# A mixer whose B products for one half pair in eight move to TensorE, and whose C products are divided anew

## The reference

```
x, z  = split(centred(inp) @ W_in)          # 1024 channels each
u     = silu(conv4(x) + conv_b)
B, C  = split(u @ W_x)                      # 16 columns each, per token
delta = softplus(u @ W_dt + b_dt)
h[d,s] = exp(delta[d] * A[d,s]) * h[d,s] + (delta[d] * u[d]) * B[s]     # token by token
y[d]  = sum_s h[d,s] * C[s]  + u[d] * D[d]
out   = (y * silu(z)) @ W_out + residual
```

## Time and profile before

| | |
|---|---|
| median of 3 runs | 5179.13 us (5176.7 to 5179.95) |
| profiled execution | 5180.01 us, span 5178.2 us |
| mean granted TensorE clock | 0.972 |
| TensorE busy | 4693.1 us, 91%, 23936 instructions |
| VectorE busy | 4584.5 us, 89%, 7668 |
| GpSimd busy | 3878.2 us, 75%, 1637 |
| ScalarE busy | 3753.9 us, 72%, 9592 |
| first scan to last scan | about 712 to 4560 us |

### The profile page before, as it was taken

The page is one execution under the profiler, slowest core; times in us unless marked ns, Lnnn a source line. Parts: engine busy times, 40 slices in busy tenths (PEclk is TensorE's granted clock), DMA queues, the critical chain, the costliest instruction groups (busy, mean ns, idle before and its releaser), DMA issues. The chain is left out here.

```text
span 5178.2 us, 79404 instructions
## 1 busy us (share of the span) xinstructions
PE 4693.1 (91%) x23936; PEld 3776.5 (73%) x23936; DVE 4584.5 (89%) x7668; ACT 3753.9 (72%) x9592; POOL 3878.2 (75%) x1637
## 2 busy tenths in 40 slices
PE   8999988898888988898899888888988989789999
PEld 6778767777777777777777777777777777668887
DVE  6777669999999999999999999999999999977775
ACT  5656557888787888888788887878888788744443
POOL 1111059999999999999999999999999999931110
PEclk9999999999999999999999999999999999989999
DMA  3222231111111111111111111111111111111111
GB/s 84 89 83 75 109 106 43 52 46 46 54 58 54 50 46 46 46 46 46 50 55 46 46 54 56 56 50 46 46 46 46 46 46 47 65 61 49 66 57 41
DMA packets 137375, 291.88 MB, mean 56 GB/s; under 512 B 23280, under 2 KB 40688, under 8 KB 136944
## 3 DMA queue, kind: packets, MB, share of 16 engines
q1 hardware_dynamic: 136944, 286.75, 16.4%
HBM read 218.53 MB, written 68.18 MB: 55 GB/s over the span
## 5 line engine op out<-in xcount | busy, mean ns | idle before, releaser
L977 POOL TENSOR_TENSOR mx_dbu<-mx_bs,mx_du 128x2048 f32<-128x2048 f32 (+1 forms) x513 | 2327.2, 4537 | 120.9 <-DVE mx_hp L1276 120.6
L1193 ACT ACTIVATE mx_ps_da<-mx_dl,mx_a 128x256 f32<-128x256 f32 x4096 | 1776.3, 465 | 99.0 <-DVE mx_hp L1276 61.6
L1276 DVE TENSOR_TENSOR_SCAN mx_ps_da<-mx_ps_da,mx_hst,mx_dbu 128x256 f32<-128x256 f32 x2016 | 1405.5, 737 | 125.1 <-ACT mx_ps_da L1193 106.9
L1276 DVE TENSOR_TENSOR_SCAN mx_hp<-mx_ps_da,mx_hst,mx_dbu 128x256 f32<-128x256 f32 x1568 | 1145.6, 731 | 11.5 <-ACT mx_ps_da L1193 11.5
L995 POOL TENSOR_TENSOR mx_hp<-mx_hp,mx_cs 128x1024 f32<-128x1024 f32 (+1 forms) x512 | 1069.4, 2095 | 1.3 <-ACT mx_hst L1117 1.3
L1396 PE MATMUL mx_ps_m<-mx_u,mx_w_dt 128*128 128x256 f32 x4096 | 930.8, 381 | 2.7 <-issue 2.7
L1396 PEld LDWEIGHTS mx_ps_m<-mx_u,mx_w_dt 128*128 128x128 f32 x4096 | 762.9, 191 | 95.7 <-issue 3.3
L1378 PE MATMUL mx_ps_m<-mx_hT,mx_w_in 128*128 128x256 f32 x2048 | 554.0, 417 | 279.7 <-DVE mx_u L1254 279.4
L1289 DVE TENSOR_TENSOR mx_hc<-mx_ps_da,mx_cs 128x512 f32<-128x512 f32 x1024 | 683.5, 667 | 2.8 <-issue 1.9
L1378 PEld LDWEIGHTS mx_ps_m<-mx_hT,mx_w_in 128*128 128x128 f32 x2048 | 395.9, 203 | 389.8 <-DVE mx_u L1254 330.5
L1426 PEld LDWEIGHTS mx_ps_y<-mx_ident,mx_hp 128*128 128x128 f32 x3584 | 444.5, 143 | 321.5 <-POOL mx_hp L995 174.8
(11 more groups left out here) (126 smaller groups left out, 7440.4 us busy)
## 6 DMA issues: line engine op xcount, KB each, us to landing
mx_bs<-bc_scratch SPq DMA_DIRECT2D x128, 512.0 KB, 4.3
mx_cs<-bc_scratch SPq DMA_DIRECT2D x128, 512.0 KB, 3.7
mx_hT<-hT_scratch SPq DMA_DIRECT2D x32, 518.0 KB, 4.1
hT_scratch<-f_h2T SPq DMA_DIRECT2D x16, 1024.0 KB, 8.9
mx_xo<-xs_scratch SPq DMA_DIRECT2D x32, 512.0 KB, 3.7
x_scratch<-mx_xo SPq DMA_DIRECT2D x32, 512.0 KB, 2.9
f_x<-in_L_attn_inp SPq DMA_DIRECT2D x12, 1024.0 KB, 6.5
xs_scratch<-f_x SPq DMA_DIRECT2D x12, 1024.0 KB, 4.3
```

Of the source, the lines that this page charges most:

```text
L977: G.tensor_tensor(dbu[:, n % NM:n % NM + k].rearrange("p n s t -> p (n s) t"), bs[:, g:g + k].rearrange("p n s t -> p (n s) t"), bcast(du[ ...
L1193: ins = A.activation(ps_da[DA_BANK[p]][:, k, :], dl[:, b % NL, :], ACT.Exp, scale=a_sb[:, b, s:s + 1])
L1276: ins = V.tensor_tensor_scan(da if in_psum(p) else hp[:, n % NH, k, :], da, dbu[:, n % NM, s, :], 0.0 if first else hst[:, b, SG * g + s:S ...
```

## The change

Pairs with g = 2 (n = 2, 6, 10, ... 30, eight a chunk) get their first half's B times delta u from TensorE:

- `turn_du`: at step 4b - 1 TensorE transposes delta u of block b (two transposes) into a `ps_m` bank; in the last chunk's last two blocks into `ps_c`.
- `copy_du`: at step 4b ScalarE copies it to SBUF (`duT`), behind the first tap and ahead of the second half's decays. The dt product of block b + 2 now waits for this copy, as it takes the same bank.
- `load_bT`, `b_diagonals`: SyncE loads the two B columns with tokens on partitions, behind the store of B and C and ahead of the spreads; at the end of step 31 ScalarE makes four diagonal matrices, identity times a B column.
- `b_times_du`: at step 4b + 1 TensorE multiplies turned delta u by the diagonals, straight into the half's `ps_da` bank, once the half three before has been scanned.
- That half's decays go to SBUF (`da_sb`), one step earlier, and its scans read decay from SBUF and B-times-du from PSUM. They write PSUM as before.
- GpSimd's double B product leaves these two states out (1536 columns, not 2048).

Apart from this `ALL_IN_PSUM` becomes empty: GpSimd makes all the C products of second halves, and `times_c_second` is no longer used.

```
-        ALL_IN_PSUM = (4, 5, 20, 21)
+        ALL_IN_PSUM = ()
+        ON_PE = 2
+        S_PE = SG * ON_PE
+        DU_TURN_AT = [NG * b - 1 for b in range(ND)]
+        DU_COPY_AT = [NG * b for b in range(ND)]
+        DIAG_AT = [-1]
+        DBU_AT = [NG * b + ON_PE - 1 for b in range(ND)]
+        def on_pe(p):
+            return p % 2 == 0 and p // 2 % NG == ON_PE
+        def du_bank(c, b):
+            return ps_c if isinstance(c, int) and c == LAST and b >= ND - 2 else ps_m[b % 2]
# SyncE, behind the wait for the stored B and C
+            def load_bT():
+                for k in range(SD):
+                    sp.dma_start(bT[:, k, :], bc_dram[S_PE + k, :].rearrange("(j p) -> p j", p=P),
+                                 allow_slow_non_contiguous=True).then_inc(s_bt, 16)
# GpSimd, times_b
+                skip = SD if on_pe(2 * n) else 0
+                G.tensor_tensor(dbu[...].rearrange("p n s t -> p (n s) t")[:, skip:, :],
+                                bs[...].rearrange("p n s t -> p (n s) t")[:, skip:, :],
+                                bcast(du[:, b % 2, :], k * SG - skip), ALU.mult).then_inc(s_m1, k)
# ScalarE
+            def copy_du(c, b):
+                act.wait_ge(s_dut, ND * c + (b + 1))
+                if not (is0(c) and b == 0):
+                    act.wait_ge(s_db, ND * c + b)
+                A.activation(duT[...], du_bank(c, b)[:, 0:T], ACT.Copy).then_inc(s_duc, 1)
+            def b_diagonals(c):
+                act.wait_ge(s_bt, 16 * SD * (c + 1))
+                if not is0(c):
+                    act.wait_ge(s_db, ND * c)
+                for j in range(TJ):
+                    for k in range(SD):
+                        ins = A.activation(bdiag[:, j, k, :], ident[:, :], ACT.Copy, scale=bT[:, k, j:j + 1])
+                ins.then_inc(s_bd, 16)
...
                     for half in range(2):
                         p = 2 * n + half
-                        if in_psum(before(p)):
+                        if on_pe(p):
+                            pass
+                        elif in_psum(before(p)):
                             keep_psum(i, p)
+                            decay(i, p)
                         else:
                             bank_scanned(i, p)
+                            decay(i, p)
...
+                    if on_pe(2 * n + 2):
+                        decay(i, 2 * n + 2)
# VectorE, scan
+                if on_pe(p):
+                    if k == 0:
+                        dve.wait_ge(s_db, ND * i + b + 1)
+                    da, db = da_sb[:, k, :], bank
+                else:
+                    da, db = bank, dbu[:, n % NM, s, :]
# TensorE; turn_du and b_times_du stand first in their steps
+                if not (is0(c) and b < 2):
+                    pe.wait_ge(s_duc, ND * c + (b - 1))          # in dt_product
+            def turn_du(c, b):
+                ...
+                    pe.wait_ge(s_zc, ND * c + (b + 3))
+                pe.wait_ge(s_du, ND * c + (b + 1))
+                for j in range(TJ):
+                    ins = M.transpose(du_bank(c, b)[:, j * P:(j + 1) * P], du[:, b % 2, j * P:(j + 1) * P], ident[:, :])
+                ins.then_inc(s_dut, 1)
+            def b_times_du(c, b):
+                n = NG * b + ON_PE
+                if b == 0:
+                    pe.wait_ge(s_bd, 16 * (c + 1))
+                pe.wait_ge(s_duc, ND * c + (b + 1))
+                pe.wait_ge(s_sc, 2 * NU * c + (2 * n - 2))
+                for j in range(TJ):
+                    ins = M.matmul(ps_da[DA_BANK[2 * n]][:, :, j * P:(j + 1) * P], duT[:, j, :], bdiag[:, j, :, :],
+                                   start=(j == 0), stop=(j == TJ - 1), skip_group_check=True)
+                ins.then_inc(s_db, 1)
```

More of the change, by code:

```diff
@@ L726, in mixer_phase @@
         yt = sb("yt", [P, 2, T])
+        da_sb = sb("da_sb", [P, SD, T])
+        duT = sb("duT", [P, TJ, P])
+        bT = sb("bT", [P, SD, TJ])
+        bdiag = sb("bdiag", [P, TJ, SD, P])
         ps_y = [ctx.enter_context(nc.psum_tensor(f"mx_ps_y{n}", [P, 512], F32)) for n in range(2)]
@@ L757, in mixer_phase @@
         s_m1 = sem("dbu_ready")
+        s_dut = sem("du_turned")
+        s_duc = sem("turned_du_copied")
+        s_bt = sem("b_columns_loaded")
+        s_bd = sem("b_diagonals_ready")
+        s_db = sem("dbu_in_psum")
         s_da = sem("da_ready")
@@ L917, in _ @@
             sp.wait_ge(s_bcd, 16)
+            load_bT()
             for g in range(NG):
@@ L1109, in log, with decay @@
                 A.activation(en[:, b % 2, :], en[:, b % 2, :], ACT.Ln, bias=1.0).then_inc(s_sp, 1)
+            def copy_du(c, b):
+                act.wait_ge(s_dut, ND * c + (b + 1))
+                if not (is0(c) and b == 0):
+                    act.wait_ge(s_db, ND * c + b)
+                A.activation(duT[:, :, :].rearrange("p j d -> p (j d)"), du_bank(c, b)[:, 0:T], ACT.Copy).then_inc(s_duc, 1)
+            def b_diagonals(c):
[6 more added lines that the diff above has]
+                ins.then_inc(s_bd, 16)
+            def decay(i, p):
+                n, half = divmod(p, 2)
+                b, g = divmod(n, NG)
+                dst = da_sb if on_pe(p) else ps_da[DA_BANK[p]]
+                for k in range(SD):
+                    s = SG * g + SD * half + k
+                    ins = A.activation(dst[:, k, :], dl[:, b % NL, :], ACT.Exp, scale=a_sb[:, b, s:s + 1])
+                ins.then_inc(s_da, 1)
             def keep(c, n):
@@ L1172, in prologue @@
                         A.preload_act_table_set("silu_and_others")
+                    for b, c in due_before(DIAG_AT, n):
+                        b_diagonals(c)
                     for k, c in due_before(U_SILU_AT, n):
@@ L1202, in body @@
                                 skip(i + s, (par + s) % 2, bb)
+                            for bb, s in due(DU_COPY_AT, n, i):
+                                copy_du(i + s, bb)
+                    if on_pe(2 * n + 2):
+                        decay(i, 2 * n + 2)
                     if n >= KEEP_LAG:
@@ L1221, in body @@
                         log(i + s, bb)
+                    for bb, s in due(DIAG_AT, n, i):
+                        b_diagonals(i + s)
                     if due(Z_SILU_AT, n, i):
@@ L1274, in scan @@
                 s = SD * half + k
-                da = ps_da[DA_BANK[p]][:, k, :]
-                ins = V.tensor_tensor_scan(da if in_psum(p) else hp[:, n % NH, k, :], da, dbu[:, n % NM, s, :],
+                bank = ps_da[DA_BANK[p]][:, k, :]
+                if on_pe(p):
[4 more added lines that the diff above has]
+                    da, db = bank, dbu[:, n % NM, s, :]
+                ins = V.tensor_tensor_scan(bank if in_psum(p) else hp[:, n % NH, k, :], da, db,
                                            0.0 if first else hst[:, b, SG * g + s:SG * g + s + 1], ALU.mult, ALU.add)
@@ L1429, in turn_onto @@
                 return ins
+            def turn_du(c, b):
+                if isinstance(c, int) and c == LAST and b >= ND - 2:
+                    pe.wait_ge(s_o, TJ * LAST)
+                    if b == ND - 1:
+                        pe.wait_ge(s_duc, ND * LAST + b)
+                else:
+                    pe.wait_ge(s_zc, ND * c + (b + 3))
[13 more added lines that the diff above has]
+                ins.then_inc(s_db, 1)
             def sum_psum_states(c, n):
@@ L1458, in prologue @@
             def prologue():
+                pe.wait_ge(s_id, 2)
                 for n in range(EARLIEST, 0):
+                    for b, c in due_before(DU_TURN_AT, n):
+                        turn_du(c, b)
                     for b, c in due_before(DT_AT, n):
@@ L1481, in body @@
                             last_out_product(j, range(2 * k, 2 * k + 2))
+                    for b, s in due(DU_TURN_AT, n, i):
+                        turn_du(i + s, b)
+                    for b, s in due(DBU_AT, n, i):
+                        b_times_du(i + s, b)
                     for part, s in due(OUT_AT, n, i):
```

12 lines of the change are left out of this document (4 added, 8 removed).

## The result

The changed kernel takes 5208.86 us (median of 5, 5205.88 to 5210.51) against 5179.13 (5176.7 to 5183.92): ratio 1.0055, 95% interval 1.0041 to 1.0070. It is slower by about 30 us. The sign was forecast, and the place; the size, +62 us, was twice too large, though the time lies inside the range given.

The account below looks back on a forecast made before the run. VectorE's in-order list, fed by ScalarE, was taken as the bound. Chunks at +2.15 us undisturbed and +2.55 disturbed, weighted 2.3, less 0.3, gave 2.0 x 31 = +62 on 5180.0: 5242 us, range 5195 to 5295.

Parts of the forecast that it names:

- place 2: Step 16, second half: input product of step 15 comes late, delaying tap and decays; VectorE stands 2.45 us.
- undisturbed chunk: A chunk without the low clock at gate 9: forecast +2.15 us in sum.
- The disturbed chunks: 12 of 29 chunks, low clock at gate 9: step 16 wait 4.15 us in place of 1.29; chunk +2.55.
- the chunk's start: Pair 0: 0.3 us gained from GpSimd, 0.2 lost waiting for second-half decays; net 0.
- the four first chunks: First chunks of a sequence: shorter scans, less cover for TensorE, but GpSimd waits go; taken at the same sum.
- SiLU blocks: Before second halves of pairs 6 and 22: VectorE's saved time becomes waiting for ScalarE's gapless chain; -0.3 to -0.4 us a chunk.
- GpSimd: Its work falls by net 4.0 us a chunk, worth 0.3 at the chunk's start and at most 0.6.
- By gate 21 TensorE has caught up: Behind step 16: B-times-du of step 17 ends some 2 us early enough; TensorE's lateness is gone by gate 21.
- Scans with exchanged operands: VectorE's scans with the two operands' places exchanged keep their present 0.73 us; +-0.02 on 16 scans is +-0.3.
- The copy: ScalarE's copy of turned delta u, between tap and second-half decays: 362 ns each, +0.36 us in place 2.
- The B column loads: SyncE's two loads ahead of the B spreads: cost nothing; a few us at each chunk's start if both took 7.4.
- the estimate: ScalarE's four diagonals of 128 columns: 0.28 us each, +1.1 a chunk, bounds 0 and 1.45.

Follow-up runs that it names:

- e1: Changed kernel with TensorE's output parts moved to steps 26, 30, 2, 8, 10, 14, 16, 18, residual and copy out to step 9: 5159.80 us.
- e9: Kernel before with TensorE's added work alone (gate products and transposes made once more, overwritten), none of its users, waits or copies: 5249.60 us.
- e7: Kernel before with the same move of output parts as e1 and nothing else: 5165.81 us.
- e10: On top of e6, the decays that go to SBUF made a step earlier still, ahead of the conv tap: 5127.97 us.
- e4: Changed kernel with Abs and ReLU of the softplus moved behind the decays of their step's second half: 5172.90 us.
- e11: Kernel of e10 with the still earlier decays only at steps 4 and 20, elsewhere as in e6: 5059.90 us.
- e2: Changed kernel with each block's transposes of delta u made twice over: 5229.67 us.
- e5: Changed kernel with ScalarE's copy of turned delta u at step 16 alone moved behind the second half's decays: 5239.42 us.
- e6: Changed kernel with both the output parts moved as in e1 and the ReLUs behind the decays as in e4: 5135.68 us.

## Why the prediction was right in kind and wrong in size

**What bounds the kernel, place 2.** Right. The forecast for an undisturbed chunk counted from the start of step 9 had input 15 at +23.85, the tap at +25.8 and the scan at +27.75; the trace has +23.96, +25.92 and +27.76. Some of that is luck: gate 9 starts 0.63 us later than before and not 0.4, and B-times-du of step 13, which therefore comes up later, waits some 0.2 us for its scan and not 0.55. The expected 2.45 us came as 2.14 at step 16 and 0.29 at step 14, where VectorE now meets a TensorE that is late with its sums. e1 shows it by taking it away.

**The steps that failed.** The mechanism held; what failed is the size of three terms of the sum: the disturbed chunks, the chunk's start put at net 0, and the four first chunks put at the same sum as the others. Forecast and measured, us for an ordinary chunk:

```
                         forecast   measured
place 2                    +2.32      +2.04    2.62, less 0.3 for fewer low-clock stretches
SiLU blocks                -0.3       -0.47
the chunk's start           0         -0.26
the other steps             0         -0.1
chunk                      +2.0       +1.22
```

Over the kernel the 27 ordinary chunks ahead of the last one brought 32 us and not 54, and the four first chunks, taken at the same sum as the others (+8), brought -1. The last chunk, at nothing, came out 2.6 shorter, and the first scan came 3.0 later (forecast 1). With 1 us less behind the last scan that is the 30 measured.

**The disturbed chunks** are the largest of the three in an ordinary chunk. The sum gave 12 of 29 chunks the low clock at gate 9 and 4.15 us of waiting. Of the twelve waits that it counted in the earlier trace rows nine stand in ordinary chunks, at about 1.28 us, and three in first chunks of a sequence, at 0.4 to 0.5. In the changed kernel no ordinary chunk is disturbed there. TensorE's idle time moved from the gates to step 6, where its transposes wait for a gate copy that ScalarE makes only behind the SiLU block; the clock falls there in 16 of the 25 chunks, and recovers before gate 9. In this kernel such a chunk takes no longer than the others (122.03 against 121.97 us). The changed kernel's TensorE row at step 6 and two windows, at step 7 and at gate 9:
```profile
2559.47 0.69 PE L1517 MATMUL mx_ps_m<-mx_ident,mx_du 128*128 128x128 f32 x2 [2.50 <-ACT mx_gy L1093]
```
```profile
2560.00:2564.00 4.00, 4.00 (x17) 3.23 (x16) 4.00 (x8) 3.35 (x11) 2.80 (x2) 0.65 0.01 2
2568.00:2572.00 4.00, 4.00 (x27) 3.63 (x26) 4.00 (x8) 2.75 (x9) 3.14 (x3) 1.00 0.01 4
```
Low-clock stretches between 900 and 4500 us went from 57 to 19. e9, which has TensorE's work but still waits 2.5 us at gate 9, keeps the low clock there in half its chunks: the price was right, the count wrong. With no disturbed chunk the term is 2.45 less the 0.46 that stood there before on the average, 1.99 and not 2.32: 0.3 to 0.4 us of the 0.8 by which the forecast was off. That the place of the idle time decides is borne out by e7, where the wait at gate 9 and the low clock there went together, and by e10, where TensorE waits 2.05 us at step 0 and 1.67 at step 6 and the low clock stands at step 0 in 14 of the 25 chunks and at step 6 in none. Not each long wait brings it, and no run moved idle time and nothing else.

**SiLU blocks: right, a little small.** Forecast -0.3 to -0.4 a chunk, measured -0.47. That the early SBUF decay brings nothing there as the change places it was right too, for the reason given: the chain holds the same instructions. Timeline of ScalarE in the changed kernel, against the earlier trace rows:
```profile
2550.78 0.88 ACT L1167 ACTIVATE mx_ps_da<-mx_dl,mx_a 128x256 f32<-128x256 f32 x2
2551.59 0.90 ACT L1167 ACTIVATE mx_da_sb<-mx_dl,mx_a 128x256 f32<-128x256 f32 x2
...
2557.21 0.47 ACT L1132 ACTIVATE mx_en<-mx_ps_m,mx_bdt 128x256 f32<-128x256 f32 x1
...
2558.15 0.87 ACT L1167 ACTIVATE mx_ps_da<-mx_dl,mx_a 128x256 f32<-128x256 f32 x2
```
From the first to the last 7.37 us; it was 7.43 between the same decays before. The decays went ahead of the block and the ReLUs stayed behind. e4 and e11 show what it takes to shorten it: move the ReLUs behind, the decays ahead of the tap.

**GpSimd: right. The chunk's start: net 0 was wrong.** The shorter product takes 3.46 us in place of 4.54, and no more was gained from it in an ordinary chunk than waits at the chunk's start. The forecast there was 0.3 us gained and 0.2 lost again before pair 0's second half. VectorE's wait at its first scan fell from 0.58 to 0.14, and 0.07 came before the second half; with smaller differences beside them the start is 0.26 us shorter.

**"By gate 21 TensorE has caught up": wrong.** In the kernel before, gate 21 starts 0.13 us behind its step's first scan, after a wait of 1.18 for the tap; in the changed kernel it starts 1.04 behind it, without a wait. TensorE waits again only at step 22, 0.49 us, for ScalarE's SiLU. That the wait at step 22 is 0.33 longer than that at step 6 doesn't show it: the difference was 0.30 before, from one more copy (0.36 us) that ScalarE makes in that block. e2 and e5 do, where more TensorE work, or later work, lengthened step 22 by 0.19 and 0.3.

**The first chunks.** The very first became 4.4 us shorter and the other three 1.3, 1.6 and 0.3 longer. "I take the same sum" failed for two reasons that their scans show. In the first chunk place 2 doesn't exist, as said above. And in all four, VectorE's waits for GpSimd at pairs 16 and 20, 0.8 to 0.9 and 1.1 to 1.2 us in the kernel before, are gone; in the three with place 2 its wait at step 16 (2.56) and new ones at steps 4, 12 and 20 outweigh that.

**Single prices.** Groups by shape, 2000 to 3000 us, changed kernel:
```profile
L1167 ACT ACTIVATE mx_ps_da<-mx_dl,mx_a 128x256 f32<-128x256 f32 x919 | 399.7, 466 | 18.3 <-DVE mx_hp L1350 9.8
...
L1350 DVE TENSOR_TENSOR_SCAN mx_ps_da<-mx_ps_da,mx_hst,mx_dbu 128x256 f32<-128x256 f32 x346 | 241.4, 748 | 0.8 <-POOL mx_dbu L1009 0.7
L1009 POOL TENSOR_TENSOR mx_dbu<-mx_bs,mx_du 128x1536 f32<-128x1536 f32 x66 | 228.1, 3456 | 31.2 <-DVE mx_hp L1350 31.2
...
L1350 DVE TENSOR_TENSOR_SCAN mx_ps_da<-mx_da_sb,mx_hst,mx_ps_da 128x256 f32<-128x256 f32 x116 | 80.1, 743 | 0.0
...
L1167 ACT ACTIVATE mx_da_sb<-mx_dl,mx_a 128x256 f32<-128x256 f32 x132 | 59.1, 496 | 0.0
...
L1148 ACT ACTIVATE mx_duT<-mx_ps_m 128x256 f32<-128x256 f32 x65 | 24.3, 373 | 0.0
...
L1157 ACT ACTIVATE mx_bdiag<-mx_ident,mx_bT 128x128 f32<-128x128 f32 x32 | 10.2, 389 | 0.0
```
Scans with exchanged operands cost the same (743 against 748), as taken. The copy was priced at 0.36 us, its own length; what follows it starts 0.26 us behind it, and e5 took 0.28 out of the wait. The B column loads land in 2.1 us and nobody waits for them.

## What to carry to other kernels

An engine that is 90% busy has its slack in places. Before work is added to it, follow its list from one wait to the next, and price the addition on the stretch where it doesn't wait; the rest of it may be free. Time taken off the busiest engine counts only if that engine isn't about to wait at the same point for a chain on another one. When such a chain is gapless, reorder it rather than relieve its neighbours: here one move of two ReLUs, one of two decays and three of output parts turned +0.55% into -2.3%. Look at the clock again after each such move: some 25 us of the last step came from low-clock stretches that went away with a shorter wait of TensorE, and no expectation had counted on them.

## What the runs showed of the hardware

- An exponential with a per-partition scale takes 496 ns into SBUF and 466 into PSUM, same source and size. The prediction leaned on an exponential with a constant scale (404 ns) and said that the rule of the Trainium skill (ScalarE: Activation LUTs, Step-by-step), PSUM being the faster destination, didn't hold; with like compared to like it does, by 30 ns. It is no gain in ScalarE's time here: the second exponential of a pair starts 400 ns behind the first into SBUF and 415 into PSUM.
- A small ACTIVATE from SBUF to SBUF isn't cheap: 128 columns with a per-partition scale take 389 ns, more than a 256-column copy out of PSUM (362 to 373). In a row they overlap and start 293 ns apart, near the 280 of the estimate.
- The idle time of TensorE costs by where it lies, and by what stands behind it. In the changed kernel the low clock behind step 6 (0.65 over 4 us) costs nothing measurable. The same low clock in e1 and e6, where an output part has moved to step 8, comes with chunks that are 0.8 and 1.5 us longer than those without it.
